# Routing's VectorE operations set one by one among the scan loop's instructions, with a second buffer for the second norm's output and a planned order of the shared PSUM bank

## The reference, cut to what matters

```python
h = _layernorm(x) * (1 + ca) + sa
dt = softplus(einsum('blr,dr->bld', x_dbl[..., :64], W_dt) + b_dt)
A_bar = exp(dt[..., None] * A);  dB_u = (dt * h)[..., None] * B_sel[:, :, None, :]
s = associative_scan(A_bar, dB_u)              # s[l] = A_bar[l] * s[l-1] + dB_u[l]
x = x + ga * (einsum('bldn,bln->bld', s, C_sel) + h * D_param)
h = _layernorm(x) * (1 + cb) + sb
probs = softmax(h @ Wg);  top_vals, top_idx = top_k(probs, 2)
gates = top_vals / sum(top_vals)
x = x + gb * sum(gates * (h @ We + be)[top_idx])
```

## Time and profile before

| | us |
|---|---|
| runs of the kernel (3) | 1138.8, 1140.89, 1141.44; median 1140.89 |
| span of the profiled execution, first to last instruction | 1135.8 |
| VectorE busy | 990.9 (87%) |
| TensorE busy | 917.4 (81%) |
| GpSimd busy | 934.9 (82%) |
| ScalarE busy | 781.4 (69%) |

### The profile page before, as it was taken

How to read it: one execution, slowest core, us unless ns; L and a number is a source line. 1 busy time by engine, 2 the same in 40 slices (tenths; PEclk the granted TensorE clock), 3 DMA queues, 4 the chain that set the end, 5 groups by cost and what they waited for, 6 DMA issues and landing times. The chain is left out here.

```text
span 1135.8 us, 14810 instructions
## 1 busy us (share of the span) xinstructions
PE 917.4 (81%) x4187; PEld 581.1 (51%) x4203; DVE 990.9 (87%) x1294; ACT 781.4 (69%) x1618; POOL 934.9 (82%) x373
## 2 busy tenths in 40 slices
PE   6336544699788988899879988899879988699998
PEld 4002111266555655456545656465536655366886
DVE  2799999999999999999999999999999999994200
ACT  5686789588967898588866897688867595442100
POOL 2376667699989999699988999799979998897553
PEclk9556665599999998899899998999889999899999
DMA  4925241627155534546174635556271716411222
GB/s 124 237 62 140 59 111 38 168 84 194 54 136 159 148 103 102 160 108 171 47 169 125 162 83 130 135 138 151 57 188 48 195 47 150 120 34 62 69 85 71
DMA packets 89793, 131.28 MB, mean 116 GB/s; under 512 B 13280, under 2 KB 73256, under 8 KB 89200
## 3 DMA queue, kind: packets, MB, share of 16 engines
q1 hardware_dynamic: 89712, 130.34, 44.8%
HBM read 54.50 MB, written 8.65 MB: 56 GB/s over the span
## 5 line engine op out<-in xcount | busy, mean ns | idle before, releaser
L1104 POOL TENSOR_TENSOR h<-h,Cr 128x2048 f32<-128x2048 f32 (+1 forms) x131 | 582.0, 4444 | 36.4 <-DVE h L989 13.1
L676 PE MATMUL ps<-xg,we 128*128 128x256 f32 x2048 | 492.5, 397 | 6.4 <-POOL xg L1138 3.6
L676 PEld LDWEIGHTS ps<-xg,we 128*128 128x128 f32 x2048 | 399.8, 199 | 88.6 <-issue 28.4
L724 ACT ACTIVATE av<-dd,An 128x512 f32<-128x512 f32 x512 | 351.0, 714 | 70.6 <-DVE h L989 64.4
L1138 POOL TENSOR_TENSOR xg<-h2T,gbc 128x1024 f32<-128x1024 f32 x128 | 303.3, 2372 | 59.0 <-PE ps L676 42.2
L976 DVE TENSOR_TENSOR ps<-ps,dd 128x512 f32<-128x512 f32 x512 | 326.4, 684 | 3.3 <-DMA dd<-src 2.8
L989 DVE TENSOR_TENSOR_SCAN h<-av,kept,ps 128x512 f32<-128x512 f32 x256 | 313.5, 1264 | 3.1 <-PE ps L569 2.5
L989 DVE TENSOR_TENSOR_SCAN h<-av,ps 128x512 f32<-128x512 f32 x256 | 298.0, 1204 | 11.1 <-PE ps L569 8.3
L569 PE MATMUL ps<-h,gam 128*32 128x512 f32 x1024 | 157.1, 741 | 53.6 <-POOL h L1104 25.2
L569 PEld LDWEIGHTS ps<-h,gam 128*32 128x32 f32 x1024 | 31.1, 124 | 134.4 <-issue 99.9
L1011 DVE TENSOR_TENSOR X<-ps,X 128x512 f32<-128x512 f32 x32 | 21.7, 679 | 64.1 <-PE ps L647 64.1
(11 more groups left out here) (105 smaller groups left out, 812.1 us busy)
## 6 DMA issues: line engine op xcount, KB each, us to landing
dd<-src SPq DMA_DIRECT2D x480, 128.0 KB, 2.4
gbc<-gates SPq DMA_DIRECT2D x128, 256.0 KB, 3.4
X<-in_x SPq DMA_DIRECT2D x8, 1024.0 KB, 6.9
out<-X SPq DMA_DIRECT2D x32, 256.0 KB, 3.5
XN<-in_x SPq DMA_DIRECT2D x7, 1024.0 KB, 7.3
dd<-src SPq DMA_DIRECT2D x16, 256.0 KB, 5.0
we<-in_We SPq DMA_DIRECT2D x2, 1024.0 KB, 10.8
XN<-in_x SPq DMA_DIRECT2D x2, 512.0 KB, 4.5
```

Source lines behind the costliest of these rows:

```text
L676: e = pe.matmul(bk[:, m * 256:(m + 1) * 256], we[:, hf, 2 * ep + e2, m * P:(m + 1) * P], xg[:, i % XG, e2, hf], start=(ep == e2 == m == hf ...
L724: act.activation(av[:, u % AS], step_of(u, 0), ACT.Exp, scale=An[:, 0, i:i + 1]).then_inc(s_a, 1)
L1104: pool.tensor_tensor(hu, hu, Cr[:, q:q + 1].to_broadcast([P, n, CH]), ALU.mult).then_inc(s_ch, n)
```

## The change

Three things are changed, and with them the numbers of the table `AT`, so that nearly every engine's order differs somewhat.

1. The steps `soft` and `top` become 17 steps `route 0` to `route 16`, each with a due time of its own that `between` puts into the next gap between two scan-loop instructions. Each operation waits only for the one whose result it needs (`after(k)`), not for the one ahead of it. Two pairs of them don't depend on each other and stand side by side.
2. `h2T` has two buffers, by the batch's parity, so that a batch's second norm waits for the expert inputs of two batches before, not of the last one.
3. `one_by_one` goes through the uses of the shared PSUM bank in order of time and moves a use, and the steps that read it, behind the reader of the use before it. A routing's 17 steps count as readers of `lT`.

The core of the diff (the table's numbers are cut to a line each way):

```diff
--- before.py
+++ after.py
...
@@ -17,34 +18,34 @@
 HS, AS, XG, GL = 8, 6, 2, 2
+RT = 16
 EPS = 1e-5
...
+          lT=0.46, soft=-2.28, softe=2.93, gT=1.19, rgT=0.76, gw=8.58, gr=27.83, xg=24.7, xgs=1.77, gl=1.81, f=-3.05,
-          rlg=1.0, lT=0.19, soft=0.37, softe=0.74, top=0.37, gT=1.19, rgT=0.76, gw=8.58, gr=27.83, xg=22.97, xgs=1.77,
...
@@ -137,6 +138,16 @@
             routed(b, t + T // 2 * (c + 1), put, {n: AT[n + "AB"[c]] for n in HALF}, (c,), (b, c))
 
 
+def between(t, i, late):
+
+    if late:
+        return t + 0.001 * i
+    p = math.floor(t)
+    gaps = (AT["mul"] + 0.025, AT["mul"] + 0.1, AT["scan"] + 0.025, AT["scan"] + 0.1)
+    i += sum(p + g < t for g in gaps)
+    return p + i // 4 + gaps[i % 4]
+
+
 def routed(b, t, put, times, halves, tag):
 
     for i, k in enumerate(k for c in halves for k in range(4 * c, 4 * c + 4)):
@@ -156,9 +167,10 @@
     put(s, "lg", *tag)
     put(s + times["rlg"], "read", "lg", *tag)
     put(s + times["lT"], "lT", *tag)
-    put(s + times["soft"], "soft", *tag)
+    late = tag == (LAST, 1)
+    for i in range(RT + 1):
+        put(between(s + times["soft"], i, late), "route", i, *tag)
     put(s + times["soft"] + times["softe"], "softe", *tag)
-    put(s + times["top"], "top", *tag)
     put(s + times["gT"], "gT", *tag)
     put(s + times["gT"] + times["rgT"], "read", "gT", *tag)
     put(s + times["gw"], "gw", *tag)
@@ -194,7 +206,31 @@
         before(b, T * (b - 1), put)
         beside(b, T * b, put)
         after(b, T * b, put)
-    return [step for _, step in sorted(at, key=lambda p: p[0])]
+    return [step for _, step in sorted(one_by_one(at), key=lambda p: p[0])]
+
+
+def followers(s):
+
+    if s[0] == "wx":
+        return [("read", *s), ("S", *s[1:])]
+    if s[0] == "lT":
+        return [("route", i, *s[1:]) for i in range(RT + 1)]
+    if s[0] == "o":
+        return [("oX", *s[1:])]
+    return [("read", *s)]
+
+
+def one_by_one(at):
+
+    time = {step: t for t, step in at}
+    last = None
+    for t, s in sorted(at, key=lambda p: p[0]):
+        if s[0] in SHARED[1:] and Bank.ring(s) is None:
+            for f in (s, *followers(s)):
+                if last is not None:
+                    time[f] = max(time[f], last + 0.01)
+                last = time[f]
+    return [(t, step) for step, t in time.items()]
 
 
 def in_bank(b, c):
...
-        h2T = sb("h2T", [P, 2, L])
+        h2T = sb("h2T", [P, 2, 2, L])
...
-        s_lg, s_lge = sem("s_lg"), sem("s_lge")
+        s_rt, s_lge = sem("s_rt"), sem("s_lge")
...
-                    if w == 1 and b >= 1 and hf == 0:
-                        act.wait_ge(s_xg, 16 * (b - 1) + 8 * (c + 1))
+                    if w == 1 and b >= 2 and hf == 0:
+                        act.wait_ge(s_xg, 16 * (b - 2) + 8 * (c + 1))
                     done(act, s)
-                    dst = hT[:, b % 2, hf, c * CH:(c + 1) * CH] if w == 0 else h2T[:, hf, c * CH:(c + 1) * CH]
+                    dst = hT[:, b % 2, hf, c * CH:(c + 1) * CH] if w == 0 else h2T[:, b % 2, hf, c * CH:(c + 1) * CH]
...
-                    act.wait_ge(s_lg, nth(s))
+                    act.wait_ge(s_rt, RT * (nth(s) - 1) + 2)
...
-            def first(s, oh, tie):
-
-                o, w = table(s, oh), table(s, 3)
-                link(dve.tensor_tensor(w, o, iw[:].to_broadcast([P, tie.shape[1], E]), ALU.mult))
-                link(dve.tensor_reduce(tie, w, AX.X, ALU.max))
-                link(dve.tensor_tensor(o, w, bc(tie), ALU.is_equal))
+            def route(s, i):
+
+                tag = s[2:]
+                use = ("lT", *tag)
+                k0, k1 = blocks(use)
+                n = (k1 - k0) // 2
+                lg = mb(use)[:, 0:256].rearrange("p (i j r) -> p j i r", i=2, j=4)[:, k0 // 2:k1 // 2, :, 0:E]
+                t0, t1, t2, t3 = (table(use, k) for k in range(4))
+                total, pe = mb(use)[:, E + k0:E + k1], pe_t[:, k0:k1]
+                top, tie, second, share = (gs[:, k, k0:k1] for k in range(4))
+                rank = iw[:].to_broadcast([P, k1 - k0, E])
+
+                def pairs(v):
+                    return v.rearrange("p (j i) e -> p j i e", i=2)
+
+                def after(k):
+                    dve.wait_ge(s_rt, RT * (nth(use) - 1) + k + 1)
+
+                if i == 0:
+                    done(dve, use)
+                    if tag[0] == 0:
+                        dve.wait_ge(s_const, 5)
+                    dve.tensor_reduce(top.rearrange("p (j i) -> p j i", i=2), lg, AX.X, ALU.max).then_inc(s_rt, 1)
+                elif i == 1:
+                    after(0)
+                    most = top.rearrange("p (j i) -> p j i", i=2).unsqueeze(3).to_broadcast([P, n, 2, E])
+                    dve.tensor_tensor(pairs(pe), lg, most, ALU.subtract).then_inc(s_rt, 1)
+                elif i == 2:
+                    after(0)
+                    most = top.rearrange("p (j i) -> p j i", i=2).unsqueeze(3).to_broadcast([P, n, 2, E])
+                    dve.tensor_tensor(pairs(t1), lg, most, ALU.is_equal).then_inc(s_rt, 1)
+                elif i == 3:
+                    after(2)
+                    dve.tensor_tensor(t3, t1, rank, ALU.mult).then_inc(s_rt, 1)
+                elif i == 4:
+                    after(3)
+                    dve.tensor_reduce(tie, t3, AX.X, ALU.max).then_inc(s_rt, 1)
+                elif i == 5:
+                    after(4)
+                    dve.tensor_tensor(t1, t3, bc(tie), ALU.is_equal).then_inc(s_rt, 1)
+                elif i == 6:
+                    after(5)
+                    dve.wait_ge(s_lge, nth(use))
+                    dve.scalar_tensor_tensor(out=t2, in0=t1, scalar=-2.0, in1=pe, op0=ALU.mult, op1=ALU.add).then_inc(s_rt, 1)
+                elif i == 7:
+                    after(6)
+                    dve.tensor_reduce(second, t2, AX.X, ALU.max).then_inc(s_rt, 1)
+                elif i == 8:
+                    after(7)
+                    dve.tensor_tensor(t0, t2, bc(second), ALU.is_equal).then_inc(s_rt, 1)
+                elif i == 9:
+                    after(7)
+                    dve.tensor_scalar(total, second, 1.0, None, ALU.add).then_inc(s_rt, 1)
+                elif i == 10:
+                    after(8)
+                    dve.tensor_tensor(t3, t0, rank, ALU.mult).then_inc(s_rt, 1)
+                elif i == 11:
+                    after(9)
+                    dve.reciprocal(share, total).then_inc(s_rt, 1)
+                elif i == 12:
+                    after(10)
+                    dve.tensor_reduce(tie, t3, AX.X, ALU.max).then_inc(s_rt, 1)
+                elif i == 13:
+                    after(12)
+                    dve.tensor_tensor(t0, t3, bc(tie), ALU.is_equal).then_inc(s_rt, 1)
+                elif i == 14:
+                    after(13)
+                    dve.tensor_tensor(pe, t0, bc(second), ALU.mult).then_inc(s_rt, 1)
+                elif i == 15:
+                    after(14)
+                    dve.tensor_tensor(t0, t1, pe, ALU.add).then_inc(s_rt, 1)
+                else:
+                    after(15)
+                    release(dve.tensor_tensor(G[:, k0:k1], t0, bc(share), ALU.mult), use)
 
             def times_b(u):
 
...
-                elif s[0] == "soft":
-                    use = ("lT", *s[1:])
-                    done(dve, use)
...
-                    emptied(dve, use)
+                elif s[0] == "route":
+                    route(s, s[1])
...
-                    pool.tensor_tensor(xg[:, i % XG], h2T[:, :, 256 * c:256 * c + 256].unsqueeze(1).to_broadcast([P, 2, 2, 256]),
+                    pool.tensor_tensor(xg[:, i % XG], h2T[:, b % 2, :, 256 * c:256 * c + 256].unsqueeze(1).to_broadcast([P, 2, 2, 256]),```

The order that results, at three places. VectorE at the routing of batch 3, in batch 4's scan loop, before (L976 is mul, L989 scan; the rows between the two are `soft` and `top`, in file order, 17 operations in a row):

```order
L976 TENSOR_TENSOR ps<-ps,dd 128x512 x2
L989 SCALAR_TENSOR_TENSOR h<-av,ps 128x512 x2
L1027 TENSOR_REDUCE gs<-ps 128x8
L1029 TENSOR_TENSOR pe_t<-ps,gs 128x64
L1030 TENSOR_TENSOR ps<-ps,gs 128x64
L966 TENSOR_TENSOR ps<-ps,iw 128x64
L967 TENSOR_REDUCE gs<-ps 128x8
L968 TENSOR_TENSOR ps<-ps,gs 128x64
```

83 lines of the change are left out of this document (29 added, 54 removed).

## The result

The changed kernel takes 1126.26 us (median of 4 runs, 1125.74 to 1129.96); the kernel before took 1139.85 us on the same chip (4 runs). The ratio is 0.9886, with a 95% interval from 0.9871 to 0.9901: faster by 1.1%. The forecast was 1122.6, range 1112 to 1140.

A forecast was written before the change was run, and what follows sets the result against it. VectorE was taken to set the loop's pace, with the loop's start and TensorE's work left at the last scan. From 1140.9: start +5.0, routing -8.8, waits -8.5, end -6.0, together -18.3, gives 1122.6 us, range 1112 to 1140.

The forecast's parts named there:

- Case A: Whole kernel: the forecast itself, each saving separate, 1122.6 us, own range 1115 to 1130; chance 0.60.
- Routing: VectorE, batches 0 to 5: single operations overlap, 2.9 us a batch instead of 4.37, -8.8 over six batches.
- D: Routing on VectorE: short operations don't overlap, each costs its whole 0.23, the 8.8 is 0: 1131.4 us; chance 0.05.
- Start: Batch 0: extra table loads and md 1 behind the transposes make scan 0 9.1 late, scan 16 5.0 late: +5.0.
- Waits: VectorE's loop waits: S -4.5, ring of h -3.0, logits -1.0, together -8.5, bounds 0 and -15.8.
- The ring's: VectorE's loop wait for the ring of h, 7.4 us before: -3.0, about half, as xg now stand singly.
- What is late next is GpSimd: Loop: once VectorE's waits shrink, GpSimd is the next engine to be late; no size given.
- End: Behind the loop: three expert steps move into it, less TensorE running dry: -7, taken as -6.0; bounds +3 and -11.5.
- Around the span: Time outside the profiled span: 5.1 us, from span 1135.8 against the median 1140.9.
- B: Loop: GpSimd takes the pace and the ring wait gives the routing's gain back: 1135.4 us; chance 0.13.
- C: Each batch's route 0 runs into the logits, VectorE waits 3.4 more six times: 1144 to 1147 us; chance 0.13.
- E: Start at full price, +9.1, with the end's gain lost: 1132.7 us; chance 0.09.

The follow-up runs named there:

- block: Changed kernel with the routing's 17 operations together at route 0's place, each waiting only for the one whose result it needs: 1135.83 us, ratio 0.9956.
- block_link: Changed kernel with the 17 routing operations together at route 0's place, each also waiting for the one ahead: 1138.12 us, ratio 0.9977.
- b_block: Changed kernel's program with the constants and order of the kernel before, routing as one block with own waits: 1139.57 us, ratio 0.9992.
- norm_first: Changed kernel with the second half's square root ahead of batch 0's first softplus and its normalizations ahead of the second: 1120.15 us, ratio 0.9824.
- b_h2t: Kernel before, in its own order, with only the second h2T buffer added: 1139.41 us, ratio 0.9991.
- ox_later: Changed kernel with oX of chunk 2 two loop instructions later in batches 1 to 6: 1127.6 us, ratio 0.9883.
- head_s: Changed kernel with the old start order (1119.3 us), plus S of chunk 0 two loop instructions later in batches 3 to 7: 1115.48 us, ratio 0.9777.
- tail_gl: tail_old with batch 6's first two gate rows asked for ahead of `out 5 3` and `ldx2 7` on SyncE's queue: 1141.89 us, ratio 1.0013.
- tail_old: Changed kernel with old constants for batch 6's routed part and batch 7, batch 6's routing one block with own waits: 1148.65 us, ratio 1.0077.

## Why the prediction was right, and where it was off

The forecast was faster by 18 us and the chip gave 13.6. Case A held: VectorE sets the pace of the loop, and overlap of short operations, the loop's waits and the end each gave something. That the time came within 3.7 us of the forecast is in part luck, since the terms were off by 7.0 on the span. Step by step, on the span:

- **Routing, -8.8 forecast, -9.7 measured** (six times 4.37 less 2.76, by the sum of the pitches), plus the 0.9 of batch 6 as forecast. The step took 0.14 for a free operation and the trace has 0.12 to 0.14; the waits inside were right too. That single operations are worth more than a block is shown by block and block_link (+9.6 and +11.9 us, of which 5.6 and 9.1 are VectorE's own time by the traces and the rest waits). That overlap alone, without the change of place, reaches the time is not shown: block against block_link is within noise, and b_block gained nothing clear. D is dead: an operation costs 0.15 or 0.25 us by whether the next needs it. In the Trainium skill the page VectorE: DVE Perf Modes, section The DRAIN you can't avoid, says that the next operation doesn't start until the pipeline is empty, but it adds that one that is not held starts earlier. The prediction took the first half alone, and these pitches bear out the second.
- **Start, +5.0 forecast, +8.7 measured.** The chain through ScalarE was nearly right: the second softplus ended at 27.06 (forecast 26.4), the transposes began at 30.59 (29.8) and from scan 0 to scan 16 there were 28.3 us (forecast 28.1). Scan 0 itself came at 47.2 instead of 43.8. Of the missing 3.4, 0.8 are these, and the other 2.6 are TensorE's: md 1 took 6.83 us where 5.04 was taken over from the earlier trace rows, and the transposes 1.94 instead of 1.09. The cause of that is the level of TensorE's clock. The trace of before shows both levels inside md 1: up to 24.7 the granted clock is 1.00 and 19 of the 32 matmuls follow each other at 0.112 us, from there it is 0.50 (1.2 GHz) and the pitch is 0.213 (columns as in the earlier trace rows):

```profile
22.50:24.70 2.20, 2.20 (x21) 2.16 (x20) 0.00 (x0) 2.19 (x3) 1.59 (x2) 1.00 0.00 0
24.70:27.60 2.90, 2.90 (x16) 2.90 (x16) 0.00 (x0) 0.09 (x1) 0.00 (x0) 0.50 0.89 181
```

In the changed kernel the pitch is 0.213 throughout. (Its trace has no entry of the clock ahead of 43.8 us, so there the level is read from the pitch.) TensorE had stood idle for 7.67 us ahead of the transposes, but the idle time isn't the cause, or not alone: in norm_first TensorE worked from 20.63 up to md 1 with no gap of over 0.1 us, and md 1 took 6.83 again. Nor is it the order alone. md 1 took 6.83 in all eight kernels with the new start or a variant of it, and 4.2 to 5.0 in five of six with the old one, but 6.99 in the sixth, b_h2t, whose start has exactly the order of before. What decides is open. Even against b_h2t, at the same level of the clock, the changed kernel's scan 64 is 7.8 late, so most of the 8.7 is the order. The waits that the old order has between scan 0 and scan 16 (4.1 us) took up most of b_h2t's delay; with scan 0 at 47.2 they are used up. The three loads cost what the trace before had for one, 1.28 to 1.30 from load to next start; the 2.66 that the Trainium skill's page ScalarE: Activation LUTs (section What ACT_TABLE_LOAD costs) gives is not seen.
- **Waits, -8.5 forecast, -3.6 measured** (what the routing leaves of the 13.3; the wait rows give -4.6). This is the term that was off most. The ring's went further than forecast, from 7.4 to 1.7 (forecast -3.0, measured -5.7), the logits' from 2.7 to 0.6; but S fell only from 5.7 to 3.8, where at most 1.2 was to be left, and oX with 5.3 is new. The step that failed is "What is late next is GpSimd": TensorE is next. ox_later shows that a wait for it that goes at oX comes back at the logits and S, and head_s that an S wait taken away comes back at the ring.
- **End, -6.0 forecast (the 0.9 of batch 6's routing was left out of the sum), -6.7 measured.** The first xg came 15.6 us after the end of scan 475 (forecast 14.9). That the sum came out is luck, for two of its terms were wrong and cancelled. The last sum was to be 0.6 later and was 4.4 later (85.0 us behind the end of scan 475 instead of 80.6). And TensorE was to run dry for up to 4.5 us more behind it, but stood idle there for 3.1 us in all, against 3.8 before; so that stretch became 11.1 us shorter, where the forecast had 7.6. tail_gl, with the three expert steps back behind the last sum, gives the same size (11.9 us). tail_old and tail_gl show that gl behind an `out` was rightly named as a cost (6.8 us there).
- **Around the span, 5.1 taken, 2.1 measured.** This error hid 3 of the 7 us by which the terms were off: luck again.

B did not come: GpSimd has 6.8 us of room a batch, and the ring's wait fell. C did not come: the logits' wait is 0.6. In block 1.8 appears in two batches, still short of the 3 us a batch that C needs. E came half: the start at nearly full price (8.7 of 9.1), but the end's gain is there as well.

## What to carry to other kernels

Short operations that depend on each other cost least with an independent instruction between them: 17 of them took VectorE 2.76 us singly, 3.70 as a block and 4.27 as a block with each waiting for the one ahead. What it is worth in the end depends on which engine is late next: putting them back into a block cost 9.6 us here, more than the 5.6 of VectorE's own time, while shortening the block in the old order gained nothing clear. Before moving a step to another place, list the activation functions in ScalarE's order and the waits ahead on each DMA queue: the place of one norm's steps at the start cost 6 us here, and two places on a queue 7. A wait that is taken away is gained only if the engine that was waited for is not late for the next one too.
